# Two experts over all tokens: first layer in split float32r, sixteen parts over routing, lists and end, closing sum on VectorE

## The chip, the cores and the metric

The kernel runs on one core of one Trainium2 chip. Five engines work side by side, each through its own queue in order: TensorE (PE; its weight loads are shown as PEld), VectorE (DVE), ScalarE (ACT), GpSimd (POOL) and SyncE (SP), which issues most transfers. They wait for each other by semaphores only. The metric is the time on the device in microseconds, from the first to the last instruction; lower is better.

## The reference

One decoder layer on 32 sequences of 128 tokens with 128 channels (4096 tokens): self-attention, cross-attention with 16 heads over 77 keys, and a layer of experts, each followed by residual and layer normalization. The part that the change touches is the last, in which each of 8 experts takes its 1024 best tokens:

```python
scores = jax.nn.softmax(xt @ Wr, axis=-1)            # 4096 x 8
G, idx = jax.lax.top_k(scores.T, k)                  # k = 1024 tokens for each expert
X_in = xt[idx]
h = jax.nn.gelu(jnp.einsum('ekd,edh->ekh', X_in, W1) + b1[:, None, :], approximate=False)
X_e = jnp.einsum('ekh,ehd->ekd', h, W2) + b2[:, None, :]
contrib = (G[..., None] * X_e).reshape(E * k, D)
out = jnp.zeros((N, D), dtype=x.dtype).at[idx.reshape(-1)].add(contrib)
```

The result is the layer normalization of x + out.

## The kernel before

**Attention** goes over 16 pairs of sequences in software-pipelined steps (`first` = -2 to 16; steps 1 to 12 are a loop over four kinds of step, so all numbers of a kind repeat). In a step TensorE works for three pairs: self-attention of the next pair (prep), cross-attention of this one (cross), and the rest of the one before (post). Results go through a ring of four PSUM banks. A unit of work takes the next bank, and waits on `ring_free` of that bank until its last content has been copied out; whoever copies it adds one to `ring_free`. The post stage ends with x2 of the pair before, which TensorE transposes into ring bank 2 (unit "x2T"); ScalarE copies it to `xall`, where the transposed x2 of all tokens gathers. Three head products (308 columns) follow, and then `cross_out(0)`, whose unit takes the same bank 2. VectorE in the same step does, in this order: maximum and subtraction of the scores of the first sequence (`cross_max(0)`, `cross_sub(0)`), their sums, small work of self-attention, `cross_max(1)`, `cross_sub(1)`, `first_norm` (first layer normalization), `cross_sum(1)`. The exponentials between are ScalarE's.

**Routing.** Softmax gates from a router product (`router`, x2T times Wr). Then each expert's 1024th best gate is found in 15 rounds of a search: VectorE counts gates above three candidates, TensorE sums the counts with one small product, VectorE takes the next candidates. After the rounds VectorE makes one-hot matrices, from which TensorE makes the lists of tokens (`make_list`).

**Experts.** Seven experts are listed: POOL gathers their rows by indirect DMA (8 of 128 rows each), TensorE transposes them, takes the first layer (8 products of 512 columns, `hidden`), ScalarE the gelu, TensorE the second layer (`second_layer`), VectorE adds the bias and multiplies by the gate (`results`), POOL scatters the rows to DRAM, SP loads them back (`landed`), and VectorE adds them to `fin`, which holds x2 (`add_landed`). The eighth expert runs over all 4096 tokens instead, with a weight of 0 where it hadn't chosen a token. It is cut into 8 parts of 512 tokens: per part four chunks of the first layer (`dense_hidden`, one product of 512 columns each) and four result steps (`dense_result`, four products of 128 columns each). Six parts run in routing, two steps per round and the others around the lists, in an order counted by `dense(n)`; two run between listed experts. ScalarE copies a part's result from PSUM, and VectorE adds it to `fin` with its weight (`dense_add`: one addition of the bias on 512 columns and four weighted additions on 128).

**End.** TensorE adds `fin` and the last landed rows in PSUM by products with the identity; VectorE takes statistics per group of four sequences, POOL the power -1/2, ScalarE normalizes 28 sequences and VectorE the last four, and SP stores eight groups.

## Time and profile before

| | |
|---|---|
| time, median of 3 runs | 589.05 us (585.27 to 589.71) |
| profiled execution, span | 585.1 us |
| TensorE busy | 549.5 us (94%) |
| VectorE busy | 417.1 us (71%) |
| ScalarE busy | 327.3 us (56%) |
| POOL busy | 260.2 us (44%) |

A matmul of float32 shows as two instructions in the profile, so that x8 stands for four products. Durations of single instructions overlap; the start of one row to the start of the next is the better measure of what a product costs. Time in brackets at the end of a row is the engine's idle time before it, with what ended it.

### The profile page before, as it was taken

The page shows a single profiled execution, that of the slowest core. Times are in us where ns is not written, and L with a number is a line of the kernel's source. Part 1 is how long each engine was busy: PE and PEld are TensorE (multiplying, and loading weights), DVE is VectorE, ACT ScalarE, POOL GpSimd, SP SyncE. Part 2 cuts the span into 40 slices and gives each one's busy share as a digit, 9 for nine tenths or more (in the row PEclk, how much of TensorE's full clock was granted, in tenths as well). Part 3 has the DMA queues.
Part 4 walks back from the last instruction along what each step waited for, and adds up shares of the span by engine and source line. Part 5 has one row for each costly group of instructions (what it writes and reads, how often), then busy time and mean ns, then how long its engine had stood idle before and what let it go on. Part 6 is the DMA issues. An engine that isn't in the chain of part 4 may idle for free.

```text
span 585.1 us, 11240 instructions
## 1 busy us (share of the span) xinstructions
PE 549.5 (94%) x3477; PEld 427.6 (73%) x3477; DVE 417.1 (71%) x1051; ACT 327.3 (56%) x670; POOL 260.2 (44%) x368
## 2 busy tenths in 40 slices
PE   8999999999999999999999898998999999999880
PEld 7868787888888788788878676566676575668530
DVE  3686786787687688668877875788758845656753
ACT  3577776767777677776767543442333525443133
POOL 4123524434352443435243430002777777777732
PEclk9999999999999999999999998998999999999985
DMA  7033442232234023423312404900223443665652
GB/s 242 2 82 91 135 117 52 96 109 97 47 115 134 25 83 115 112 50 115 104 60 65 150 10 144 304 2 11 55 57 106 138 129 121 191 194 163 221 185 108
DMA packets 62151, 63.43 MB, mean 108 GB/s; under 512 B 11809, under 2 KB 48930, under 8 KB 61858
## 3 DMA queue, kind: packets, MB, share of 16 engines
q1 hardware_dynamic: 58096, 55.37, 30.8%
q0 software_dynamic: 3584, 7.58, 4.6%
q8 instruction: 20, 0.33, 0.2%
q14 instruction: 17, 0.14, 0.1%
q10 hardware_dynamic: 434, 0.02, 0.0%
HBM read 36.85 MB, written 26.08 MB: 108 GB/s over the span
## 4 chain that ended last, share of the span: by engine, by line
PE 77%; DVE 13%; ACT 4%; issue 2%; POOL 1%; DMA 1%; POOLq 0%; DVEq 0%; ACTq 0%
PE PS L1577 17%; PE PS L1635 10%; PE PS L1607 9%; PE PS L1908 8%; PE PS L1930 7%; PE PS L1623 5%; PE PS L1821 4%; PE PS L1831 4%; DVE pc L1395 2%; DVE csum L1158 1%; ACT shared L891 1%; DVE cmax L1147 1%; PE PS L1681 1%; PE PS L1675 1%; PE PS L1667 1%
## 5 line engine op out<-in xcount | busy, mean ns | idle before, releaser
L767 POOL TENSOR_TENSOR pn<-pc,crcp 128x512 f32<-128x512 f32 (+1 forms) x93 | 80.4, 891 | 69.3 <-DVE crcp L1161 69.3
L1035 ACT ACTIVATE shared<-PS,b1T 128x512 f32<-128x512 f32 x88 | 60.5, 687 | 85.7 <-PE PS L1821 49.5
L807 POOL DMA_INDIRECT shared<-table,idx x56 | 54.3, 970 | 64.5 <-DVE idx L1402 48.0
L1607 PE MATMUL PS<-shared,x1T 128*128 128x512 f32 (+1 forms) x192 | 72.4, 513 | 1.2 <-ACT x1T L906 1.0
L817 POOL DMA_INDIRECT spread<-pn,idx x56 | 62.0, 1107 | 17.6 <-issue 15.6
L1607 PEld LDWEIGHTS PS<-shared,x1T 128*128 128x128 f32 x192 | 35.0, 189 | 37.6 <-issue 35.2
L862 ACT ACTIVATE shared<-PS 128x308 f32<-128x308 f32 x120 | 47.5, 428 | 25.5 <-PE PS L1577 25.2
L1147 DVE TENSOR_REDUCE cmax<-PS 128x16 f32<-128x1232 f32 x31 | 44.7, 1441 | 20.8 <-PE PS L1607 20.4
L1158 DVE TENSOR_REDUCE csum<-pc 128x16 f32<-128x1232 f32 x31 | 44.4, 1431 | 19.4 <-ACT pc L874 19.4
L1908 PE MATMUL PS<-pT,w 128*128 128x512 f32 x112 | 53.6, 611 | 3.3 <-ACT pT L1030 3.3
L1930 PEld LDWEIGHTS PS<-w,shared 128*128 128x128 f32 x448 | 51.7, 192 | 3.6 <-issue 3.1
L1930 PE MATMUL PS<-w,shared 128*128 128x128 f32 x448 | 52.9, 276 | 0.1
L862 ACT ACTIVATE pT<-PS 128x512 f32<-128x512 f32 (+2 forms) x97 | 44.0, 526 | 14.2 <-PE PS L1623 14.1
L786 POOL TENSOR_TENSOR rs<-ve,mhalf 128x2 f32<-128x2 f32 x16 | 11.2, 702 | 79.9 <-DVE ve L1217 79.9
L1152 DVE TENSOR_TENSOR pc<-PS,cmax 128x1232 f32<-128x1232 f32 x31 | 44.6, 1437 | 0.6
L1577 PE MATMUL PS<-cT_hi,heads_hi 128*128 128x308 f32 x128 | 43.8, 342 | 1.0 <-DVE r L1186 0.7
L874 ACT ACTIVATE pc<-pc 128x1232 f32<-128x1232 f32 x31 | 38.2, 1231 | 10.0 <-DVE pc L1152 9.6
L1908 PEld LDWEIGHTS PS<-pT,w 128*128 128x128 f32 x112 | 17.8, 189 | 32.8 <-ACT shared L1035 19.8
L1623 PE MATMUL PS<-ident,pn 128*128 128x128 f32 (+1 forms) x320 | 40.7, 274 | 0.9 <-ACT shared L891 0.5
L1831 PEld LDWEIGHTS PS<-w2d,shared 128*128 128x128 f32 x256 | 32.8, 196 | 10.2 <-issue 9.6
L1635 PE MATMUL PS<-VOeven,pT 128*128 128x128 f32 (+1 forms) x320 | 38.5, 276 | 1.0 <-ACT pT L862 0.5
L1635 PE MATMUL PS<-shared,pT 128*128 128x128 f32 (+1 forms) x320 | 38.5, 275 | 0.5 <-ACT pT L862 0.5
(209 smaller groups left out, 1208.1 us busy)
## 6 DMA issues: line engine op xcount, KB each, us to landing
spread<-zeros SPq DMA_DIRECT2D x112, 128.0 KB, 2.0
shared<-spread SPq DMA_DIRECT2D x56, 256.0 KB, 4.3
xboth<-in_x SPq DMA_DIRECT2D x16, 256.0 KB, 2.7
w<-in_W SPq DMA_DIRECT2D x2, 1792.0 KB, 9.2
rest<-stage SPq DMA_DIRECT2D x56, 52.0 KB
table<-x SPq DMA_DIRECT2D x16, 128.0 KB, 1.9
fin<-table SPq DMA_DIRECT2D x1, 2048.0 KB, 18.2
out_x<-fin SPq DMA_DIRECT2D x8, 256.0 KB, 2.0
```

The costliest lines, as they stand in the source:

```text
L767: pool.tensor_tensor(pn[:, e, at_pn:at_pn + n * (b - a)].rearrange("p (h k) -> p h k", h=n), pc[:, e, :].rearrange("p (h k) -> p h k", h=H ...
L807: pool.indirect_dma_start(xg[:, e % 3, h, :], None, table, bass.IndirectOffsetOnAxis(ap=idx[:, e, h:h + 1], axis=0)).then_inc(gathered[e % ...
L817: pool.indirect_dma_start(spread[e], bass.IndirectOffsetOnAxis(ap=idx[:, e, h:h + 1], axis=0), ye[:, e % 2, h, :], None).then_inc(scattere ...
L862: act.activation(dst, src, ACT.Copy).then_inc(free[bank_of(at, name)], 1)
L1035: act.activation(hid[:, c, 512 * h:512 * h + 512], PS[:, HID_BANKS[k % len(HID_BANKS)], :], ACT.Gelu, bias=b1T[:, bias:bias + 1]).then_inc ...
L1577: i = pe.matmul(bank, a, b, start=(n == 0), stop=(n == len(pairs) - 1))
L1607: i = pe.matmul(PS[:, n, 0:b - a], x1T[:, e, :], A[:, 2 * A_SLOT[phase] + e, a:b], start=True, stop=True)
L1623: i = pe.transpose(bank[0:rows, (c - a) * P:(c - a + 1) * P], pn[:, e, n:n + rows], ident[:, :])
L1635: i = pe.matmul(bank[:, 0:P], pT[0:rows, e, c * P:(c + 1) * P], VO[par][0:rows, e, c, :], start=(c == 0), stop=(c == CH - 1))
L1831: i = pe.matmul(PS[:, 1 + h, s * P:(s + 1) * P], hid[:, c, 512 * h + s * P:512 * h + (s + 1) * P], w2d[:, c, :], start=(c == 0), stop=(c = ...
L1908: pe.matmul(PS[:, HID_BANKS[k % len(HID_BANKS)], :], w1[:, e, c * P:(c + 1) * P], xeT[:, 512 * h:512 * h + 512], start=True, stop=True).th ...
L1930: i = pe.matmul(y_bank(e, h, s), hid[:, c, (4 * h + s) * P:(4 * h + s + 1) * P], w2[:, e, c, :], start=(c == 0), stop=(c == FC - 1))
```

## The change

- Two experts (6 and 7) run over all tokens, six are listed. There are 16 parts: part u takes tokens of group u // 2 and expert 6 + u % 2. Eight run in routing, one each after listed experts 1 and 3, six at the end.
- The first layer of these parts is done in split float32r: `xall` is kept as a high and a low half (float32r each), as is w1d, and a chunk is three products, high x high, low weights x high, high weights x low. The router is done in the same way.
- So x2T is taken out of its ring bank in two steps: ScalarE writes the high half and no longer frees the bank; VectorE (`x2T_rest`) subtracts it from the bank, writes the low half, and frees the bank. It stands behind `first_norm`.
- POOL splits Wr at the start and w1d after attention.
- In routing, `dense(2 + r % 2)` follows each round's product: two steps in even rounds, three in odd ones.
- The results of parts go to a buffer `yd` of eight. At the end VectorE takes `dense_add` of parts 10 to 14, the landed rows of the last expert, statistics and normalization from `fin` in SBUF in an order written out; TensorE's closing sum is gone. The last part is added straight from PSUM.
- Buffers of attention now lie where later ones are, so that memory suffices.

```diff
-LISTED = E - 1
-DENSE = E - 1
-GROUPS_OF_FOUR = B // 4
-IN_ROUTING = 6
+LISTED = E - 2
+DENSES = E - LISTED
+PARTS = DENSES * B // 4
+IN_ROUTING = 8
+BETWEEN = {1: IN_ROUTING, 3: IN_ROUTING + 1}
+AT_END = IN_ROUTING + len(BETWEEN)
+KEPT = 8
...
+            pool.wait_ge(w1d_in, 16)
+            pool.tensor_copy(w1d[0][:, :, :], w1d_raw).then_inc(w1d_split, 1)
+            pool.wait_ge(w1d_split, 1)
+            pool.tensor_tensor(w1d[1][:, :, :], w1d_raw, w1d[0][:, :, :].bitcast(F32), ALU.subtract).then_inc(w1d_split, 1)
...
                 if post:
-                    copy(at, "x2T", xall[:, bass.ds(2 * (p - 1), 2), :].rearrange("p e t -> p (e t)"), bank("x2T")[:, 0:2 * P])
+                    ring_wait_full(act, at, "x2T")
+                    act.activation(xall[0][:, bass.ds(2 * (p - 1), 2), :].rearrange("p e t -> p (e t)"), bank("x2T")[:, 0:2 * P],
+                                   ACT.Copy).then_inc(x2T_hi, 1)
...
+                def x2T_rest():
+
+                    wait(dve, x2T_hi, p)
+                    ring_wait_full(dve, at, "x2T")
+                    two = bass.ds(2 * (p - 1), 2)
+                    dve.tensor_tensor(xall[1][:, two, :].rearrange("p e t -> p (e t)"), ring[bank_of(at, "x2T")][:, 0:2 * P],
+                                      xall[0][:, two, :].rearrange("p e t -> p (e t)").bitcast(F32),
+                                      ALU.subtract).then_inc(free[bank_of(at, "x2T")], 1)
...
                 if prep:
                     first_norm()
+                if post and cross:
+                    x2T_rest()
...
+            add_landed(LISTED - 2, 0, B // 4)
+            dense_add(10)
+            dense_add(11)
+            dense_add(12)
+            add_landed(LISTED - 1, 0, B // 4)
+            fin_stats(0)
+            fin_stats(1)
+            dense_add(13)
+            fin_stats(2)
+            fin_stats(3)
+            fin_stats(4)
+            fin_stats(5)
+            dense_add(14)
+            last_bias()
+            fin_stats(6)
+            last_add()
+            fin_stats(7)
...
-                        i = pe.matmul(small[:, b * E:(b + 1) * E], xall[:, b, :], wr[:, :], start=True, stop=True)
+                        i = products(small[:, b * E:(b + 1) * E], ((xall[0][:, b, :], wrs[0][:, :]), (xall[0][:, b, :], wrs[1][:, :]),
+                                                                   (xall[1][:, b, :], wrs[0][:, :])))
...
+                w_hi, w_lo = [t[:, d, c * P:(c + 1) * P] for t in w1d]
+                x_hi, x_lo = [t[:, 4 * g:4 * g + 4, :].rearrange("p b t -> p (b t)") for t in xall]
+                products(PS[:, HID_BANKS[k % len(HID_BANKS)], :],
+                         ((w_hi, x_hi), (w_lo, x_hi), (w_hi, x_lo))).then_inc(hid_full, 1)
...
-                    dense(2)
+                    dense(2 + r % 2)
...
+            for u in range(AT_END, PARTS):
+                if u < AT_END + 2:
+                    pe.wait_ge(ye_done, 2 * (LISTED - 1) + u % 2 + 1)
+                else:
+                    pe.wait_ge(dense_out, u - 1)
+                for n in range(FC):
+                    if u + 1 < PARTS:
+                        dense_hidden(end_hidden(u + 1) + n, u + 1, n)
+                    dense_result(end_hidden(u), u, u % 2, n)
```

VectorE in a looped attention step, before, from the statistics of `first_norm` (writing mv and ve) to the sum of the second sequence's exponentials (csum); pc holds the exponentials:

```order
L1210 BN_STATS st<-PS 128x6
L174 REGISTER_ALU
L1214 BN_AGGR mv<-st 128x2 [waits ln1_steps]
L1214 BN_AGGR mv<-st 128x2
L1217 TENSOR_SCALAR ve<-mv 128x2 [waits ln1_steps]
L1158 TENSOR_REDUCE csum<-pc 128x16 [waits cexp_done]
L1161 RECIPROCAL crcp<-csum 128x16 [waits csum_done]
```

The same place of the changed kernel:

```order
L1242 BN_STATS st<-PS 128x6
L177 REGISTER_ALU
L1246 BN_AGGR mv<-st 128x2 [waits ln1_steps]
L1246 BN_AGGR mv<-st 128x2
L1249 TENSOR_SCALAR ve<-mv 128x2 [waits ln1_steps]
L177 REGISTER_ALU [waits x2T_hi]
L1210 ISA [waits ring_full2]
L1210 TENSOR_TENSOR xall_lo<-PS,xall_hi 128x256
L1181 TENSOR_REDUCE csum<-pc 128x16 [waits cexp_done]
L1184 RECIPROCAL crcp<-csum 128x16 [waits csum_done]
```

Between the last operation of `first_norm` and the sum the subtraction has come in, with two register and wait instructions ahead of it.

TensorE in the changed kernel's looped step, the transposes of x2 (x_0); before, these rows and the next read the same but for their line numbers:

```order
L1834 MATMUL PS<-ident,x_0 128x128 [waits ring_free2,x2_done]
L1834 MATMUL PS<-ident,x_0 128x128
```

Behind them on TensorE, from the last of the head products (cT and heads) to the first products of `cross_out(0)` (out of pT):

```order
L177 REGISTER_ALU
L1597 MATMUL PS<-cT_hi,heads_hi 128x308 [waits ring_free1]
L1597 MATMUL PS<-cT_lo,heads_hi 128x308
L1597 MATMUL PS<-cT_hi,heads_lo 128x308
L1695 MATMUL PS<-shared,pT 128x128 [waits ring_free3,ring_free2]
L1695 MATMUL PS<-shared,pT 128x128 x3
L1695 MATMUL PS<-shared,pT 128x128 [waits ring_free0]
```

The first product of `cross_out(0)` waits on ring_free2, the bank that the x2T transposes filled; it was freed by ScalarE's copy and is now freed by VectorE's subtraction.

TensorE at the end of routing, before: from the last quarter of list 1 (out of pc and tokens) to the transposes of the first expert's gathered rows (in the tile named shared):

```order
L1889 MATMUL PS<-tokens,pc 128x16 [waits onehot_done]
L1889 MATMUL PS<-tokens,pc 128x16 x7
L1831 MATMUL PS<-w2d,shared 128x128 x12
L1900 MATMUL PS<-ident,shared 128x128 [waits gathered0_0,w2_in,w1_in]
```

And in the changed kernel a chunk and a result behind the list (four products of w2d are one result step):

```order
L1597 MATMUL PS<-xall_hi,w1d_hi 128x512 [waits hid_done]
L1597 MATMUL PS<-xall_hi,w1d_lo 128x512
L1597 MATMUL PS<-xall_lo,w1d_hi 128x512
L1898 MATMUL PS<-w2d,shared 128x128 [waits hid_done,dense_out]
L1898 MATMUL PS<-w2d,shared 128x128 x3
```

Its last chunk, the results behind it, and the first expert's transposes:

```order
L1597 MATMUL PS<-xall_hi,w1d_hi 128x512 [waits hid_done]
L1597 MATMUL PS<-xall_hi,w1d_lo 128x512
L1597 MATMUL PS<-xall_lo,w1d_hi 128x512
L1898 MATMUL PS<-w2d,shared 128x128 x4
L1898 MATMUL PS<-w2d,shared 128x128 [waits hid_done,dense_out]
L1898 MATMUL PS<-w2d,shared 128x128 x15
L1969 MATMUL PS<-ident,shared 128x128 [waits gathered0_0,w2_in,w1_in]
```

Three result steps (x12) have become four chunks and eight result steps; between the two pieces the pattern of a chunk and a result goes on.

VectorE at the end, before, from the last landed rows to the first statistics:

```order
L1460 TENSOR_TENSOR fin<-fin,shared 128x512 [waits landed_added,landed_in6]
L1460 TENSOR_TENSOR fin<-fin,shared 128x512 [waits landed_added,landed_in7]
L1506 BN_STATS stf<-PS 128x6 [waits fin_full,landed_added]
L1506 BN_STATS stf<-PS 128x6 x3
L1509 BN_AGGR mvf<-stf 128x2 [waits chain]
```

And in the changed kernel, from `dense_add(12)` into the landed rows of the last expert:

```order
L1469 TENSOR_TENSOR yd<-yd,b2b 128x512 [waits dense_added,landed_added,dense_out]
L1471 SCALAR_TENSOR_TENSOR fin<-yd,weight,fin 128x128 [waits chain]
L1471 SCALAR_TENSOR_TENSOR fin<-yd,weight,fin 128x128 x3
L1487 TENSOR_TENSOR fin<-fin,shared 128x512 [waits landed_added,landed_in0,dense_added]
L1487 TENSOR_TENSOR fin<-fin,shared 128x512 [waits landed_added,landed_in1]
```

The landed rows of the last expert now stand behind the addition of part 12, and the statistics read `fin` and wait for both.

## Rows read from the trace of the kernel before

**Rows 1.** Busy time by stage: window, then engines' busy us and count, PEclk, DMA, GB/s.

```profile
100.00:200.00 100.00, 99.70 (x639) 83.91 (x638) 76.36 (x173) 72.80 (x162) 41.44 (x70) 1.00 0.30 90
...
362.00:366.00 4.00, 3.45 (x6) 1.64 (x7) 2.35 (x11) 1.74 (x2) 0.00 (x0) 0.50 1.02 409
```

**Rows 2.** Timeline, TensorE: start us, us, line, tiles, count, idle before. Starts of experts.

```profile
419.82 3.89 PE L1908 MATMUL PS<-pT,w 128*128 128x512 f32 x8 [0.74 <-ACT pT L1030]
...
484.23 3.89 PE L1908 MATMUL PS<-pT,w 128*128 128x512 f32 x8 [1.26 <-ACT pT L1030]
...
504.05 7.66 PE L1908 MATMUL PS<-pT,w 128*128 128x512 f32 x16
...
519.56 7.66 PE L1908 MATMUL PS<-pT,w 128*128 128x512 f32 x16
...
545.89 4.11 PE L1930 MATMUL PS<-w,shared 128*128 128x128 f32 x32
```

**Rows 3.** Timeline, TensorE: cross_out(0) of two steps, and scores(0) of a next.

```profile
209.54 2.40 PE L1635 MATMUL PS<-VOeven,pT 128*128 128x128 f32 x20
...
214.46 2.33 PE L1607 MATMUL PS<-shared,x1T 128*128 128x512 f32 x6
...
271.86 2.40 PE L1635 MATMUL PS<-shared,pT 128*128 128x128 f32 x20
```

**Rows 4.** Timeline, VectorE: cmax(0), end of first_norm, csum(1), next cmax(0); another step's.

```profile
197.02 1.44 DVE L1147 TENSOR_REDUCE cmax<-PS 128x16 f32<-128x1232 f32 x1 [0.92 <-PE PS L1607]
...
211.06 0.17 DVE L1217 TENSOR_SCALAR ve<-mv 128x2 f32<-128x2 f32 x1
211.14 1.43 DVE L1158 TENSOR_REDUCE csum<-pc 128x16 f32<-128x1232 f32 x1
...
216.83 1.44 DVE L1147 TENSOR_REDUCE cmax<-PS 128x16 f32<-128x1232 f32 x1 [0.34 <-PE PS L1607]
...
272.80 0.17 DVE L1217 TENSOR_SCALAR ve<-mv 128x2 f32<-128x2 f32 x1
```

**Rows 5.** Timeline, VectorE, routing: a copy of 128x256 from PSUM.

```profile
363.25 0.42 DVE L1331 COPY gatesT<-PS 128x256 f32<-128x256 f32 x1 [0.84 <-PE PS L1855]
```

**Rows 6.** Chain that ended last, in order of time: start us, us, engine, line.

```profile
454.46 3.64 PE PS L1821 x8
...
459.35 3.89 PE PS L1908 x8
...
463.23 3.57 PE PS L1831 x32
```

**Rows 7.** Timeline, TensorE: float32r value products, single instructions.

```profile
201.39 0.48 PE L1577 MATMUL PS<-heads_hi,cmain_hi 128*128 128x512 f32 x1
201.71 0.40 PE L1577 MATMUL PS<-heads_hi,cmain_lo 128*128 128x512 f32 x1
201.95 0.39 PE L1577 MATMUL PS<-heads_lo,cmain_hi 128*128 128x512 f32 x1
```

**Rows 8.** Timeline, TensorE: the count product that closes two rounds.

```profile
391.20 0.18 PE L1864 MATMUL PS<-count,group 128*128 128x7 bf16 x1
...
393.23 0.18 PE L1864 MATMUL PS<-count,group 128*128 128x7 bf16 x1
```

**Rows 9.** Timeline, VectorE: dense add, landed add, statistics, last normalization.

```profile
439.14 0.68 DVE L1443 TENSOR_TENSOR xall<-xall,b2b 128x512 f32<-128x512 f32 x1
...
440.95 0.68 DVE L1443 TENSOR_TENSOR xall<-xall,b2b 128x512 f32<-128x512 f32 x1
...
536.25 4.89 DVE L1460 TENSOR_TENSOR fin<-fin,shared 128x512 f32<-128x512 f32 x8
...
571.62 0.88 DVE L1506 BATCH_NORM_STATS2 stf<-PS 128x6 f32<-128x128 f32 x4
...
573.10 0.88 DVE L1506 BATCH_NORM_STATS2 stf<-PS 128x6 f32<-128x128 f32 x4
...
575.71 1.36 DVE L1517 TENSOR_SCALAR fin<-PS,mvf,rsf 128x128 f32<-128x128 f32 x4 [1.06 <-POOL rsf L834]
```

More of the change, by code:

```diff
@@ L227, in decoder_layer @@
             wheadsT = set_up_only.enter_context(nc.sbuf_tensor("wheadsT", [P, 3, HEADS // 2, P], F32))
-        xall = sb("xall", [P, B, P])
+        xall_hi = sb("xall_hi", [P, B, P], F32R)
         wT = sb("wT", [P, 3, P])
         wvo = sb("wvo", [P, 2, P + 1])
+        xall_lo = sb("xall_lo", [P, B, P], F32R)
+        xall = [xall_hi, xall_lo]
+        wr = sb("wr", [P, E])
+        wrs = [sb(f"wr_{k}", [P, E], F32R) for k in ("hi", "lo")]
+        b1T = sb("b1T", [P, E * FC])
         with ExitStack() as attention:
@@ L243, in decoder_layer @@
             VOeven = part("VOeven", [P, 2 * HKP])
+            xboth = [part(f"xboth{k}", [P, 2, 2, P]) for k in range(2)]
+            xin = [t[:, 0, :, :] for t in xboth]
+            xT = [t[:, 1, :, :] for t in xboth]
+            cin = part("cin", [P, 4 * KEYS])
+            crin = part("crin", [P, REST])
+            crest = [part(f"crest_{k}", [P, REST], F32R) for k in ("hi", "lo")]
+            stage = part("stage", [REST, 2, 4 * P])
+            xbo = part("xbo", [P, 2, P])
+            qT = part("qT", [P, 2, P])
+            vs = part("vs", [P, 2, P + 1])
+            skey = part("skey", [P, 2])
+            smin = part("smin", [P, 2])
+            pself = part("pself", [P, 2, P])
+            ssum = part("ssum", [P, 2])
+            srcp = part("srcp", [P, 2])
+            pselfT = part("pselfT", [P, 2, P])
+            st1 = part("st1", [P, 2, 6])
+            mv1 = part("mv1", [P, 2, 2])
+            ve1 = part("ve1", [P, 2])
+            rs1 = part("rs1", [P, 2])
+            x1 = [part(f"x1_{k}", [P, 2, P]) for k in range(2)]
+            x1T = part("x1T", [P, 2, P])
         MT = [t[:, 0:HEADS, :] for t in halves]
@@ L348, in decoder_layer @@
         nmf = sb("nmf", [P, B])
-        w1d = sb("w1d", [P, F])
-        w2d = sb("w2d", [P, FC, P])
-        weight = sb("weight", [P, B])
+        w1d = [sb(f"w1d_{k}", [P, DENSES, F], F32R) for k in ("hi", "lo")]
+        w2d = sb("w2d", [P, DENSES, FC, P])
+        weight = sb("weight", [P, DENSES, B])
         self_in = sem("self_in")
@@ L483, in hidden_before, with end_hidden @@
         def hidden_before(e):
-            return FC * IN_ROUTING + 2 * FC * e + FC * sum(e > k for k in TAIL)
-        TAIL = {1: IN_ROUTING, 2: IN_ROUTING + 1}
+            return FC * IN_ROUTING + 2 * FC * e + FC * sum(e > k for k in BETWEEN)
+        def end_hidden(u):
+            return hidden_before(LISTED) + FC * (u - AT_END)
         CONSTS = 21
@@ L805, in gather @@
                     pool.wait_ge(ye_done, 2 * (e - 2))
-                for h in range(first, end):
+                for h in range(SB):
                     pool.indirect_dma_start(xg[:, e % 3, h, :], None, table,
@@ L1473, in _ @@
                 make_idx(e)
-            for e in range(LISTED - 1):
+            for e in range(LISTED):
                 if e + 3 < LISTED:
@@ L1484, in _ @@
                     add_landed(e - 2, B // 8, B // 4)
-                if e < 2:
-                    for k in range(IN_ROUTING // 2 * e, IN_ROUTING // 2 * (e + 1)):
-                        dense_add(k, 0)
-                if e - 1 in TAIL:
-                    dense_add(TAIL[e - 1], B // 4 * (e - 1))
-            add_landed(LISTED - 3, 0, B // 4)
-            last_results()
-            add_landed(LISTED - 2, 0, B // 4)
+                for u in ((0, 1, 2), (3, 4, 5), (6, 7), (8,), (), (9,))[e]:
+                    dense_add(u)
             def fin_shift(c):
@@ L1533, in _, with products @@
             pe.wait_ge(consts, 4)
+            def products(bank, pairs):
+                for n, (a, b) in enumerate(pairs):
+                    i = pe.matmul(bank, a, b, start=(n == 0), stop=(n == len(pairs) - 1))
+                return i
             def set_up_unit(k):
@@ L1573, in done @@
                     i.then_inc(full[bank_of(at, name)], 1)
-                def products(bank, pairs):
-                    for n, (a, b) in enumerate(pairs):
-                        i = pe.matmul(bank, a, b, start=(n == 0), stop=(n == len(pairs) - 1))
-                    return i
                 def heads(which):
```

300 lines of the change are left out of this document (139 added, 161 removed).

## The prediction

> **What bounds the kernel now.** I read the busy time by stage first: between 100 and 200 us TensorE works 99.70 of 100 us at a granted clock of 1.00 [rows 1]. So whatever TensorE gets to do or to wait for during attention is paid in full. Then the timelines, engine by engine, and the chain of waits for prices. Up to 362 us there is attention (16 steps, one per pair of sequences), up to 419.82 routing [rows 2], then seven listed experts, whose last second layer starts at 545.89 and takes about 4.1 us [rows 2], so TensorE's own work on experts is over at 550.0. The last 35.1 of the 585.1 us are scatter, landing, closing sum and normalization. This tail is what the six closing parts are laid over.
>
> The profiled execution takes 585.1 us, which is the fastest of the three times; their median is 589.05. I make the sum against 585.1 and carry the difference over at the end.
>
> **A. The new x2T handover, 12 looped steps.** Before, ScalarE copied the transposed x2 out of its ring bank right after TensorE had written it, and cross_out(0) started at 209.54 without idle time ahead of it [rows 3]. Now ScalarE writes only the high half, and the bank is given back by VectorE's subtraction, which stands behind first_norm. The order excerpt of TensorE's looped step shows who waits: the first matmul of cross_out(0) asks for ring_free2, the bank of x2T, and only three head products lie between. In the step shown VectorE's last operation of first_norm starts at 211.06 and the next one at 211.14 [rows 4]. The subtraction is 128x256 with one operand in PSUM; its nearest row is a 128x256 copy from PSUM at 0.42 us [rows 5]. In the loop two register and wait instructions stand in front of it, which I put at 0.1. So the bank is free at 211.14 + 0.1 + 0.42 + 0.05 for the semaphore = 211.7, against 209.54: a wait of 2.2 us.
>
> Is the wait made good later? VectorE's work from cmax(0) at 197.02 to 211.14 is one chain: cmax, subtraction, ScalarE's exp, sum, and then back to back without a gap. It starts when TensorE's scores(0) end. From cross_out(0) to the scores of the next step TensorE needs 214.46 - 209.54 = 4.9 us and the scores another 2.3 [rows 3]; nothing of it can move ahead. So the loop of one step becomes 197.02 to 211.7 on VectorE, then 7.3 us on TensorE to the next cmax(0) (216.83 before, [rows 4]): 22.0 us where there were 19.8. The wait comes back in every step. The other looped steps repeat four kinds; one kind has an earlier first_norm, 272.80 against a cross_out(0) at 271.86 [rows 3, 4], which gives 0.94 + 0.08 + 0.57 = 1.6. So 9 x 2.1 + 3 x 1.6 = 23.7, less 0.5 for small waits for x1 that vanish behind it: **+23.2** (bounds 20 and 26).
>
> **B. The last four steps and the gates.** Here heads and prep run out, TensorE waits for VectorE anyhow, and the new wait replaces part of another. Nothing: 0; all of it: 4 x 2.1 = 8.4. I take half, **+4**. The 32 router products become three of 8 columns each; the trace has no such product, and I leave them at nothing, with 1.4 us to either side. POOL's split of w1d (two operations on 1024 columns) is wanted when TensorE begins its dense chunks; POOL stands idle there (0.00 of 4 us, [rows 1]) and has its last attention work behind it before the gates are made. Nothing, at most 1.
>
> **C. Price of a part.** A float32 chunk of the first layer takes 3.64 / 4 = 0.91 us, a result step (four 128x128 products) 3.57 / 4 = 0.89 [rows 6]. A split chunk is three float32r products of 512 columns. The same shape stands in the value products, at 201.39, 201.71 and 201.95 [rows 7], so 0.32 for the first one after float32 work, then 0.23 each: 0.78 after float32, 0.69 otherwise. One chunk and one result: 0.78 + 0.89 = 1.67 us, against 1.80 before. A whole part is 6.7 us.
>
> The Trainium skill (TensorE: Matmul & The Clock Gate, Back-to-back issue gap) gives N / 2.4 + 2.5 ns for a warm matmul, 216 ns for 512 columns, and knows no extra after a float32 product. By it a chunk would be 0.65 us, and about 30 chunks on the path some 4 us cheaper in all, an estimate. The rows here show 0.23 and 0.32.
>
> **D. Rounds.** A round runs 391.20 to 393.23 = 2.03 us [rows 8] and VectorE sets it; TensorE has one chunk and one result, 1.83. With 1.67 the even rounds stay at 2.03. Odd rounds have three steps: chunk, result, chunk 2.45 + 0.04 (four rounds, +0.46) or result, chunk, result 2.56 + 0.04 (three rounds, +0.57): +3.55. In the first two rounds TensorE's products ran at half clock (0.50 between 362 and 366, [rows 1]) and held VectorE up; cheaper chunks give back 0.9. **+2.65** (0 to 3.6).
>
> **E. End of routing.** While lists are made VectorE's one-hots set the pace, so cheaper chunks bring nothing. Behind list 1 there were 3 result steps, 2.67 us; now 4 chunks and 8 results: 4 x 0.78 + 8 x 0.89 = 10.24. **+7.6**. Hidden(0,0) starts at 427.4 instead of 419.82 (the other shifts apart).
>
> **F. Listed stretch.** It was 550.0 - 419.82 = 130.2. Experts 0 and 1 took 459.35 - 419.82 = 39.5 [rows 2, 6], and in them are four dense chunks from 454.46 and a 1.25 us wait for ScalarE behind them, 4.9 in all; with cheaper chunks ScalarE's gelus end 0.6 earlier: 38.9. e2 loses its own chunks, so it is like e3 before, 504.05 - 484.23 = 19.8. e3 is e4 before (519.56 - 504.05 = 15.5) plus chunks and wait (4.45): 20.0. e4 is 15.5 + 3.57 = 19.1. e5: 7.5 + 3.57 + four chunks 3.05 + 3.57 = 17.7. Sum 115.4, end at 542.8. So one expert less saves **-14.8**.
>
> **G. The end.** Parts 10 to 15 follow. TensorE needs 5 x 6.7 + 3.57 = 37.1, end 579.9. But VectorE's order decides: dense_add(12) stands ahead of add_landed(5), and needs part 12: 542.8 + 3 x 6.7 + 0.85 (ScalarE's copy) = 563.75. Earlier work of VectorE (add_landed(4), parts 10, 11) is 4.9 + 2 x 1.81 = 8.5 us and fits in front. The last expert's landed rows were ready, at latest, 571.62 - 550.0 = 21.6 us behind its second layer [rows 2, 9]; now that is 564.4, and they are asked for at 565.6. So part 12 is what is waited for. From there VectorE has, by [rows 9]: dense_add 1.81 three times (12, 13, 14); eight landed adds 4.9; stats of groups 0 to 6 at 1.48, 10.4 in all; last_bias and last_add 2.3; then from stats(7) to the end of the last normalization 577.07 - 573.10 = 3.97. Sum 27.0, so 590.8. From the last normalization to the end of the span it was 585.1 - 577.07 = 8.0, and stays. End 598.8, which is **+13.7** against 585.1. ScalarE's 28 normalizations start near 577 and end before VectorE.
>
> **Sum.** 585.1 + 23.2 + 4 + 2.65 + 13.7 = 628.7. (E and F are inside G.) Without the x2T handover the same change would be 602: eight more parts cost more than one listed expert and the covered tail give back.
>
> **Rivals.**
> - *The bank is free in time* (10%): VectorE's place behind first_norm isn't reached late after TensorE's new rhythm, or the delay is absorbed before the next scores. For it: VectorE idles 0.34 to 0.92 us ahead of cmax(0) [rows 4]. Against: that idle is behind the wait, not before it. Then 585.1 + 2.65 + 13.7 = 601.5, up to 606.
> - *More than the plain wait* (7%): a late cross_out(0) makes the second normalization late, which goes over POOL and VectorE to the x2 that the next transposes need. If it falls behind by 1 us more in each of 13 steps: 642 and more.
> - *Not slower* (3%): TensorE takes up the handover and the extra steps in idle time, so that only the covered tail counts. The tail after the last expert was 35.1; all of B, D, E would have to vanish: 419.8 + 115.4 + 37.1 + about 13 for a tail bound by TensorE = 585. It decides once TensorE has 40 us of idle before 550; but it is idle 585.1 - 549.5 = 35.6 us in the whole span, most of it in the tail. Against it speaks the 99.70 of 100 too.
>
> **Numbers.** Forecast 80%: 628.7 on the profiled execution; the median of before lies 4 us over its profile, so I name 631. The range holds the bounds of A to G (20 to 26, 0 to 8.4, 0 to 3.6, some 3 us for G and 1.4 for the router) and a little of the second rival: 616 to 643. About 1% is what a measurement of this kernel tells from no change. Faster 0.01, same 0.03, slower 0.96.
>
> **What would show it.** Right: in the looped steps a wait of cross_out(0) of about 2 us released by VectorE's subtraction, cmax(0) to cmax(0) near 22 us where it was 19.8; attention some 25 us longer; TensorE idle in steady steps for the first time. Rounds alternating 2.03 and 2.5. Twelve steps of 10.2 us ahead of the first transposes. At the end VectorE without a gap from dense_add(12) on, TensorE done some 11 us before the last normalization. Wrong: if attention keeps its length, A falls and the time is about 602. If VectorE has gaps at the end, a landing or ScalarE sets it. If a chunk comes to 0.65 us, C is off by 3 to 4 us.

## The result, and the profile after

| | before | changed |
|---|---|---|
| median, us | 587.16 (4 runs) | 644.25 (4 runs, 642.9 to 645.85) |
| profiled execution, span | 585.1 | 642.1 |
| TensorE busy | 549.5 (94%) | 579.9 (90%) |
| VectorE busy | 417.1 (71%) | 429.1 (67%) |

The changed kernel takes 1.095 of the time before (95% interval 1.088 to 1.101), 57 us more. I had forecast 631 (616 to 643): the direction was right, the size 13 us short. By stages of the two profiled executions, where the boundaries are the first maximum of a step on VectorE, the first and the last count product of the search, hidden(0,0), and the end of the last listed second layer:

| stage | before | changed | difference | forecast |
|---|---|---|---|---|
| to the last maximum of attention | 346.5 | 377.9 | +31.3 | +27.2, with the next row |
| last maximum to first count product | 19.9 | 29.9 | +10.0 | |
| 14 rounds of the search | 28.8 | 32.7 | +3.8 | +2.65 |
| last count product to hidden(0,0) | 24.6 | 32.3 | +7.7 | +7.6 |
| hidden(0,0) to the last listed second layer | 130.2 | 116.2 | -13.9 | -14.8 |
| from there to the end | 35.1 | 53.2 | +18.1 | +20.9 |

First the waits of TensorE over the whole execution (line waited for: us in all, times, the longest), the changed kernel:

```profile
PE PS L1695 <- DVE xall_lo L1210: 27.5, 14, 3.0
PE PS L1977 <- ACT pT L1047: 3.3, 3, 1.3
```

L1695 is cross_out, L1210 the new subtraction. Before, the same product started without idle time ahead of it [rows 3]. Its place in one step on TensorE (start us, us, line, tiles, count, idle before), changed kernel:

```profile
225.13 0.30 PE L1597 MATMUL PS<-cT_hi,heads_lo 128*128 128x308 f32 x1
227.50 2.50 PE L1695 MATMUL PS<-VOeven,pT 128*128 128x128 f32 x20 [2.07 <-DVE xall_lo L1210]
```

and on VectorE, the end of first_norm, the subtraction, the sum; before, the second row was not there [rows 4]:

```profile
226.79 0.17 DVE L1249 TENSOR_SCALAR ve<-mv 128x2 f32<-128x2 f32 x1
227.02 0.42 DVE L1210 TENSOR_TENSOR xall_lo<-PS,xall_hi 128x256 f32 x1
227.36 1.42 DVE L1181 TENSOR_REDUCE csum<-pc 128x16 f32<-128x1232 f32 x1
```

The head product's last piece starts at 225.13, the subtraction ends at 227.44, and cross_out(0) starts at 227.50. The next step's first maximum shows the period: 212.75 to 234.68 us, 21.9 where it was 19.8.

In two of the twelve looped steps the period went to 24.9 us, where the forecast's terms give 21.1 + 2.1 = 23.2. There the same products run slower behind the wait. TensorE in one of them, and then the windows around it (window, busy us of PE, PEld, DVE, ACT, POOL with counts, granted clock, DMA share, GB/s):

```profile
249.30 4.12 PE L1695 MATMUL PS<-shared,pT 128*128 128x128 f32 x20 [2.04 <-DVE xall_lo L1210]
```

```profile
248.00:250.00 2.00, 0.70 (x5) 0.70 (x6) 1.76 (x6) 1.04 (x4) 0.70 (x1) 0.93 0.00 0
250.00:252.00 2.00, 2.00 (x11) 2.00 (x11) 1.40 (x4) 0.00 (x0) 1.04 (x2) 0.50 0.00 0
252.00:254.00 2.00, 2.00 (x12) 1.81 (x12) 0.50 (x2) 0.00 (x0) 1.52 (x3) 0.72 0.00 0
```

Twenty instructions take 4.12 us that took 2.40 before [rows 3], at a granted clock of 0.50, the lower of the two levels (1.2 and 2.4 GHz), after 2 us in which TensorE stood idle.

### The profile page after: what moved, and what is told of

Its sections match the earlier page's. It is cut to its first block, busy times and chain, and to the rows that moved or that the text cites. A ratio compares the mean times of both kernels' runs of the same rounds, so it can differ in the third digit from the quotient of the medians.

```text
span 642.1 us, 11830 instructions
## 1 busy us (share of the span) xinstructions
PE 579.9 (90%) x3741; PEld 477.1 (74%) x3741; DVE 429.1 (67%) x1086; ACT 347.7 (54%) x699; POOL 247.2 (38%) x356
## 3 DMA queue, kind: packets, MB, share of 16 engines
q1 hardware_dynamic: 54640, 51.17, 26.4%
## 4 chain that ended last, share of the span: by engine, by line
PE 51%; DVE 32%; issue 8%; ACT 6%; DMA 1%; DVEq 1%; SPq 0%; POOLq 0%; POOL 0%
PE PS L1597 15%; PE PS L1695 8%; PE PS L1990 6%; PE PS L1977 6%; DVE cmax L1170 6%; PE PS L1898 6%; PE PS L1667 6%; DVE csum L1181 3%; DVE pc L1175 3%; ACT pc L889 3%; DVE pc L1430 2%; DVE PS L1272 1%; DVE shared L1264 1%; DVE above L1375 1%; DVE PS L1236 1%
## 5 line engine op out<-in xcount | busy, mean ns | idle before, releaser
L1052 ACT ACTIVATE shared<-PS,b1T 128x512 f32<-128x512 f32 x112 | 77.0, 688 | 99.2 <-PE PS L1597 71.0
L827 POOL DMA_INDIRECT shared<-table,idx x48 | 46.3, 965 | 73.1 <-DVE idx L1437 59.4
L1898 PEld LDWEIGHTS PS<-w2d,shared 128*128 128x128 f32 x512 | 65.4, 194 | 5.2 <-issue 1.0
L1898 PE MATMUL PS<-w2d,shared 128*128 128x128 f32 x512 | 67.4, 279 | 0.0
L837 POOL DMA_INDIRECT spread<-pn,idx x48 | 51.7, 1078 | 26.2 <-DVE pn L1450 13.1
L1695 PE MATMUL PS<-shared,pT 128*128 128x128 f32 (+1 forms) x320 | 44.6, 302 | 12.4 <-DVE xall_lo L1210 11.9
L1695 PE MATMUL PS<-VOeven,pT 128*128 128x128 f32 (+1 forms) x320 | 40.7, 284 | 16.1 <-DVE xall_lo L1210 15.6
L1695 PEld LDWEIGHTS PS<-shared,pT 128*128 128x128 f32 (+1 forms) x320 | 42.3, 215 | 14.4 <-DVE xall_lo L1210 13.6
L1695 PEld LDWEIGHTS PS<-VOeven,pT 128*128 128x128 f32 (+1 forms) x320 | 38.5, 198 | 18.1 <-DVE xall_lo L1210 17.3
L1977 PE MATMUL PS<-pT,w 128*128 128x512 f32 x96 | 46.1, 612 | 3.3 <-ACT pT L1047 3.3
L1990 PEld LDWEIGHTS PS<-w,shared 128*128 128x128 f32 x384 | 44.4, 192 | 3.0 <-issue 2.9
L1990 PE MATMUL PS<-w,shared 128*128 128x128 f32 x384 | 45.1, 276 | 0.0
```

The costliest lines, as they stand in the source:

```text
L1052: act.activation(hid[:, c, 512 * h:512 * h + 512], PS[:, HID_BANKS[k % len(HID_BANKS)], :], ACT.Gelu, bias=b1T[:, bias:bias + 1]).then_inc ...
L1695: i = pe.matmul(bank[:, 0:P], pT[0:rows, e, c * P:(c + 1) * P], VO[par][0:rows, e, c, :], start=(c == 0), stop=(c == CH - 1))
L1898: i = pe.matmul(y, hid[:, c, 512 * h + s * P:512 * h + (s + 1) * P], w2d[:, u % DENSES, c, :], start=(c == 0), stop=(c == FC - 1))
L1977: pe.matmul(PS[:, HID_BANKS[k % len(HID_BANKS)], :], w1[:, e, c * P:(c + 1) * P], xeT[:, 512 * h:512 * h + 512], start=True, stop=True).th ...
L1990: i = pe.matmul(PS[:, 1 + h, s * P:(s + 1) * P], hid[:, c, (4 * h + s) * P:(4 * h + s + 1) * P], w2[:, e, c, :], start=(c == 0), stop=(c = ...
```

## The experiments

Ratios are against the kernel before on the same chip, with 95% intervals. The first four runs below were made on a chip on which the kernel before took 623.1 us; there TensorE waited in short pieces with no releaser (issue) in the stretch of the experts, so these runs are read by their stages in attention and gates, which show no such pieces. Of the kernel before there is no profile on that chip, but the run with one expert has its attention and gates unchanged: they took 293.8 and 19.8 us there. "Attention" below is from step 1's first maximum to the last maximum: 293.9 us before (52.60 to 346.51), 325.9 in the changed kernel (51.96 to 377.85).

### The subtraction earlier in VectorE's queue

```diff
                 if cross and first < PAIRS - 1:
                     cross_sub(1)
+                    if post:
+                        x2T_rest()
...
-                if post and cross:
+                if first == PAIRS - 1:
                     x2T_rest()
```

> The changed kernel, with VectorE's subtraction of x2T moved from behind first_norm to right behind cross_sub(1), 2.9 us earlier in its queue; nothing else. Theory A (the late return of ring bank 2 is what makes attention longer: 31 us by the time of cmax in the last step, 585.1 against 642.1 in span): the bank is free within 0.2 us of when cross_out(0) wants it, the 2 us waits in front of cross_out(0) go, first_norm comes 0.35 us later in a step; cmax(0) to cmax(0) about 20 and 21.3 us, attention 26 to 31 us shorter, span 613 to 616. With the waits the stretches at half clock in two of the looped steps (about 1.7 us each) should go too. Rival (the added subtraction and ScalarE's writing of the high half make the steps longer by themselves): less than 10 us comes back, over 630.

Measured: 1.041 (1.036 to 1.046) of the kernel before on its chip. Attention took 299.9 us: 26 of the 32 us are back. The two steps at half clock are gone as well (periods 21.5 us). In the list of TensorE's waits the line of cross_out no longer stands among the largest; of its 14 waits for the subtraction one is left:

```profile
PE PS L1960 <- issue: 9.8, 13, 1.9
PE PS L1979 <- ACT pT L1047: 4.9, 3, 2.4
PE PS L1992 <- issue: 4.6, 5, 1.2
PE PS L1979 <- ACT shared L1052: 2.2, 1, 2.2
...
PE PS L1697 <- DVE xall_lo L1210: 1.2, 1, 1.2
```

So theory A holds; the rival does not. The span of 647.7 us is no test of the 613 to 616, because of the chip; the run with both fixes below is. The gates stretch was not mended: 30.7 us.

### The late return alone, on the kernel before

```diff
-                    copy(at, "x2T", xall[:, bass.ds(2 * (p - 1), 2), :].rearrange("p e t -> p (e t)"), bank("x2T")[:, 0:2 * P])
...
                 if prep:
                     first_norm()
+                if post and cross:
+                    x2T_copy()
```

> The kernel before, in float32 and with one expert over all tokens as it was; only the copy of x2T out of ring bank 2 is taken from ScalarE and given to VectorE behind first_norm, where the changed kernel has its subtraction. Theory A: that alone brings the wait of about 2.1 us ahead of cross_out(0) into each looped step, cmax(0) to cmax(0) near 21.9 and 23.3 us, one step in four up to 24.9 where the clock falls; time 610 to 617. Rival (the wait is harmless without the other parts of the change): under 595.

Measured: 1.062 (1.058 to 1.066), 40 us more on that chip. Attention 327.2 us, 33.2 more than before, with no high and low half, one expert over all tokens, and nothing else changed but that the copy is VectorE's work and no longer ScalarE's. TensorE's waits:

```profile
PE PS L1640 <- DVE xall L1220: 27.1, 14, 3.0
```

This is nearly the same sum, over the same 14 steps, as in the changed kernel. Who frees the bank, and when, makes the attention part of the loss. (Of the 40 us, 33 are attention; I did not settle what the other 7 are on that chip.)

### The router with one product per block

```diff
-                        i = products(small[:, b * E:(b + 1) * E], ((xall[0][:, b, :], wrs[0][:, :]), (xall[0][:, b, :], wrs[1][:, :]),
-                                                                   (xall[1][:, b, :], wrs[0][:, :])))
+                        i = products(small[:, b * E:(b + 1) * E], ((xall[0][:, b, :], wrs[0][:, :]),))
```

> The changed kernel with one product per block of the router (high x high) in place of three: the two with a low half are left out, so gates are less exact. From the last cmax of attention to the first count product it took 29.9 us in the changed kernel and 19.9 before. Theory R (64 more router products of 0.11 us at full and 0.21 us at half clock, and a granted clock of 0.50 over some 23 us around them): 32 products take some 4 us where 96 took about 17; 7 to 10 us come back, 632 to 635. Rival R2 (the 10 us come from VectorE's x2T_rest standing ahead of the last sums, a wait of 2.98 us, and from waits for bank 2): 3 us or less come back, over 639.

Measured: 1.072 (1.069 to 1.075) on that chip. From the last maximum to the first count product 21.4 us, where it was 29.9 and, before, 19.9: 8.5 of the 10 us are back, as theory R said. (Other executions with all 96 products took 27.1 and 30.7 us there, so the gain is 5.7 to 9.3 us.) R2 falls by this and again below. What a product costs is in two rows of the changed kernel's TensorE, first at full, then at half clock:

```profile
376.81 0.25 PE L1597 MATMUL PS<-wr_hi,xall_hi 128*128 128x8 f32 x1
376.92 0.25 PE L1597 MATMUL PS<-wr_lo,xall_hi 128*128 128x8 f32 x1
...
381.40 0.35 PE L1597 MATMUL PS<-wr_hi,xall_hi 128*128 128x8 f32 x1
381.61 0.35 PE L1597 MATMUL PS<-wr_lo,xall_hi 128*128 128x8 f32 x1
```

Start to start 0.11 and 0.21 us. The kernel before had the router in float32; these rows of its TensorE were there to be read:

```profile
356.41 2.74 PE L1645 MATMUL PS<-wr,xall 128*128 128x8 f32 x24
359.00 0.42 PE L1772 MATMUL PS<-ident,x 128*128 128x128 f32 x2
```

24 instructions in 2.59 us from the start of one row to the start of the next: 0.108 each, two for a block, 0.22. Three products of 0.111 are 0.33. So 32 blocks cost 32 x 0.12 = 3.8 us more at full clock. That is not the whole: this run has half the router instructions of the kernel before and still takes 1.5 us longer. The rest goes with the clock. Over this stretch the mean granted clock was 0.86 before, 0.64 in the changed kernel and 0.77 here, and the executions with three products follow it: 25.1 us at 0.80 (with the wide weights below), 27.1 at 0.71, 29.9 at 0.64, 30.7 at 0.62. What takes the clock down there stays open.

### One expert, its last two parts at the end

```diff
-        TAIL = {1: IN_ROUTING, 2: IN_ROUTING + 1}
+        TAIL = {}
...
+            for c in range(FC):
+                dense_hidden(last + c, IN_ROUTING, 0, c)
+            pe.wait_ge(ye_done, blocks_through(LISTED - 1, SB - 1))
+            for g in range(IN_ROUTING, B // 4):
+                for n in range(FC):
+                    if g + 1 < B // 4:
+                        dense_hidden(last + FC * (g + 1 - IN_ROUTING) + n, g + 1, (g + 1) % 2, n)
+                    dense_result(last + FC * (g + 1 - IN_ROUTING), g, g % 2, n)
```

(with statistics and normalization from fin, as in the changed kernel)

> The kernel before, with seven listed experts and one over all tokens in float32 as it was, but the last two of its 8 parts are moved from between listed experts to the end, and the closing sum goes to VectorE (landed rows and statistics group by group from fin, additions of parts 6 and 7 ahead of group 6). It takes from the change only its use of the tail. Each part between experts cost TensorE 3.64 + 1.26 + 3.57 = 8.5 us, so the last listed second layer ends 17 us earlier, near 533; rows land 17 us earlier, at 544 to 553; parts 6 and 7 take TensorE until about 549. VectorE then has 8 x 2.1 + 2 x 1.8 = 20.4 us from 544, the last normalization is at 567, end at 575 (572 to 580). Rival (landing or VectorE's chain gives it all back): 583 or more. If one expert over all tokens laid into the tail is faster and two are slower, the tail holds two or three parts of 6.4 to 7.2 us, not six.

Measured: 1.022 (1.018 to 1.027). TensorE's waits there had 29 us put down to issue, in the stretch of the listed experts:

```profile
PE PS L1939 <- issue: 14.1, 27, 1.2
PE PS L1898 <- issue: 12.7, 14, 1.9
```

So it was run again, on a chip on which the kernel before took 585.9 us.

> The kernel before with its last two parts in the tail, as in the run before. There it was 1.022 of the kernel before where the sum said 0.983, with 29 us of idle time of TensorE put down to issue between 440 and 580 us. Theory I (that idle time, which this chip or its instruction supply brings into straight code, hit it harder): where the kernel before takes 587 us, TensorE has none of it and the kernel takes 574 to 580. Theory V (the tail has no room: landing or VectorE's chain binds): it is at 587 or over there too.

Measured: 593.5 us, 1.012 (1.008 to 1.016). Theory I falls: without the issue waits it is slower too. V is right about what bounds the tail: VectorE waits for the first landed rows until 559.32 and then runs without a gap up to the usual 1.06 us ahead of the last normalization, while TensorE is done at 563.9. But the sum had counted that chain, and the tail took 41.8 us where the sum had 42 (533 to 575). What the sum had wrong is the listed stretch: it did not get shorter at all. Windows over it, before and then this kernel (columns as above):

```profile
419.82:550.00 130.18, 127.34 (x852) 88.65 (x852) 84.87 (x153) 51.94 (x79) 100.14 (x97) 1.00 0.45 137
```

```profile
419.17:549.31 130.14, 118.81 (x773) 82.88 (x774) 81.17 (x143) 45.74 (x69) 100.33 (x97) 0.96 0.44 138
```

TensorE has 8.5 us less busy time (and slower products, at a mean clock of 0.96), and the stretch still takes 130.1 us. The waits of TensorE name what took the place of its work, the gathered rows:

```profile
PE PS L1909 <- DMA shared<-table,idx: 10.7, 6, 4.2
```

and POOL has the two groups that make them, in this kernel (line, form, count, busy us, mean ns, idle before):

```profile
L817 POOL DMA_INDIRECT spread<-pn,idx x56 | 60.6, 1082 | 17.1 <-issue 15.8 <-DVE pn L1434 0.6 <-DVE pn L1421 0.6
L807 POOL DMA_INDIRECT shared<-table,idx x56 | 55.2, 985 | 64.7 <-DVE idx L1408 48.2 <-issue 16.2 <-DVE pn L1434 0.3
```

Each is followed by 0.30 us of issue, so a listed expert costs POOL 8 x (1.08 + 0.98 + 0.6) = 21.3 us (the first gathers lie ahead of the stretch), more than the 15.5 us that TensorE needs for an expert without a dense part [rows 2]. In the stretch of the kernel before, POOL's idle time ahead of these two groups is 27.7 us of issue and 2.3 us of waits for VectorE. With seven listed experts POOL is a second bound at 130 us, and the two dense parts between them were free work in its shadow. The tail then held them at a price, 41.8 us where there were 35.1: the end moved from 585.1 to 591.1.

### Once more the changed kernel, on that chip

> The changed kernel once more, unchanged, so that the others of this call have it on their own chip: in the call before, the kernel before took 623 us where it took 587 in the first comparison, with TensorE idle in short pieces that nothing released (put down to issue) in the stretch of the listed experts alone. Attention and routing have no such pieces. Expected: a ratio near 1.095 where the kernel before takes 587; cmax(0) to cmax(0) 21.9, 24.9, 23.4, 21.9 as before.

Measured: 646.2 us, 1.102 (1.098 to 1.107). The waits for the bank are again 27.5 us in 14 steps, but the periods differ from run to run: six of the looped steps had stretches at half clock here, two in the first profile, and attention took 330.6 us, not 325.9. The wait is fixed; what the clock adds to it is not.

### The router's products widened

```diff
-                        i = products(small[:, b * E:(b + 1) * E], ((xall[0][:, b, :], wrs[0][:, :]), (xall[0][:, b, :], wrs[1][:, :]),
+                        i = products(small[:, b * E:b * E + WIDE], ((xall[0][:, b, :], wrs[0][:, :]), (xall[0][:, b, :], wrs[1][:, :]),
```

> The changed kernel, with the router's weights padded by zeros from 8 to 64 columns: the same 96 products, each with 8 times the columns, written over each other in rising order so that each block keeps its 8. Theory K (the granted clock falls to half around the narrow products, and that is most of the 10 us that the last attention step and the gates take longer): it stays at 1.00 for most of that stretch, and 4 to 7 us come back although no product is saved, 637 to 640 where the changed kernel takes 644. Theory N (it is the number of products alone, 0.11 us each): no gain, and wider products can only be slower, 644 to 647.

Measured: 645.6 us, 1.100 (1.095 to 1.105), against 646.2: no difference that can be measured. Its gates stretch took 25.1 us at a mean clock of 0.80, the unchanged kernel's on the same chip 27.1 at 0.71. That leans the way of theory K, with 2 us and not 4 to 7; since unchanged code gave 27.1, 29.9 and (with the early subtraction) 30.7 us there, it is not shown. What the run does show is that eight times the columns cost nothing.

### Both fixes together

The subtraction behind cross_sub(1), as in the first diff, and the wide router; and in the last step that has them, the last sums go ahead:

```diff
                 if first == PAIRS - 1:
                     last_sums(0)
                     last_sums(1)
+                    x2T_rest()
```

> The changed kernel with x2T's subtraction right behind cross_sub(1) in the steps, behind the last sums in the last step that has them, and with the router's weights 64 columns wide. Expected from the two effects: 26 to 28 us from attention and 5 to 8 from the gates, 609 to 613 where the changed kernel takes 644; what then remains over the kernel before, 20 to 26 us, is rounds (3.8), the end of routing (7.7) and the listed stretch with the end (9.5), and attention about 2. Under 600 would mean that those weren't priced right.

Measured: 613.9 us, 1.047 (1.042 to 1.052), where the changed kernel took 646.2: 32 us back. Attention 300.0 us, gates 25.1 us. Putting the last sums in front brought nothing to the gates stretch (25.1 in both this and the wide router alone), which speaks against R2 once more. What remains over the kernel before, 27.5 us by the spans (612.6 and 585.1): attention 6.1, gates 5.2, rounds 3.0, end of routing 9.2, listed stretch and end 4.1.

### Who frees the bank

```diff
+                    wait(act, x2T_lo, p)
+                    act.activation(x2c[:, :], bank("x2T")[:, 0:2 * P], ACT.Copy).then_inc(free[bank_of(at, "x2T")], 1)
```

> On top of the run with both fixes (613.9 us, steps of 20.6, 20.1, 21.5, 21.6 us): ScalarE copies the transposed x2 a second time, as float32 into SBUF, and that frees ring bank 2; VectorE's subtraction reads the copy and stands where the changed kernel has it, behind first_norm. Theory A' (only the time at which the bank comes back matters, not where the subtraction stands): no wait of 2 us ahead of cross_out(0), steps as with both fixes or 0.3 us shorter, since first_norm no longer has the subtraction in front of it: 609 to 614. Rival (a subtraction behind first_norm delays the sum and the second normalization as much): steps over 21.5 us throughout, over 625.

Measured: 613.9 us, 1.044 (1.037 to 1.052). Attention 300.0 us, the same as with the early subtraction, although the subtraction is again behind first_norm. So its place costs nothing once the bank no longer hangs on it; theory A' holds. The 6 us that attention still takes over the kernel before stay too, in both variants, so the order does not make them. The 0.42 us that each of 15 steps has more on VectorE come to 6.3 us; that these are the cause fits in size but was not tested.

### Two steps a round

```diff
-                    dense(2 + r % 2)
+                    dense(2)
```

> On top of both fixes: two dense steps in each round of the search, where odd rounds had three. The seven steps move behind list 1. From the rows: rounds get 7 x 0.55 = 3.8 us shorter, the end of routing 4 x 0.78 + 3 x 0.81 = 5.5 us longer, so 1 to 2 us slower, 615 to 616; a gain would mean that steps behind list 1 are hidden.

Measured: 616.5 us, 1.047 (1.039 to 1.055), not to be told from 613.9 by that interval. By stages: rounds 29.2 us where both fixes had 31.8, end of routing 37.9 where it had 33.8. The trade is 2.6 against 4.2 where 3.8 against 5.5 had been worked out. In the rounds the first one took 0.7 us more here (2.79 and 2.09); the end of routing took 32.3 to 33.8 us in other runs with the same code there, the chip of the first four left out.

### The router in two products

```diff
+                        pe.matmul(small[:, 2 * E * b:2 * E * (b + 1)], xall[0][:, b, :], wrs[:, 0:2 * E], start=True, stop=False)
+                        i = pe.matmul(small[:, 2 * E * b:2 * E * b + E], xall[1][:, b, :], wrs[:, 0:E], start=False, stop=True)
```

> On top of both fixes, but with the router in two products in place of three (high x with high and low weights side by side in 16 columns, low x with the high weights) and a copy and an addition on VectorE per batch of gates. Theory N (number of products, 0.11 us each at full and 0.21 at half clock): 32 products less, of which some 24 lie on the path, 2.6 to 5 us, less 2 x 0.6 us of VectorE: 1.5 to 4 us faster, 610 to 612. If narrow products pull the clock down, part of it goes back: no change.

Measured: 614.2 us, 1.043 (1.037 to 1.049): no gain. TensorE was busy for 3.0 us less in the gates stretch (19.1 against 22.1), but that took 25.1 us as before, at a clock of 0.73 in place of 0.80, and VectorE had 2.7 us more. The run also gives up the wide weights, so it does not tell the count of products from their columns.

### All of it

The last diff and the one on who frees the bank, together.

> bank_by_act and router_two together, the best that I know to make of two experts over all tokens: 606 to 611, still some 20 us over the kernel before, which is what one more expert over all tokens costs (51 us of TensorE for 8 parts, against one listed expert and about 17 us of a tail better filled).

Measured: 613.5 us, 1.040 (1.033 to 1.047), 2.5 us over the range that I expected. Its gates stretch was the shortest of the versions with the full router, 22.8 us at a clock of 0.82. No version with two experts over all tokens comes within 20 us of the kernel before, and the kernel before stays the fastest of all that ran.

## Why the prediction was right, and where it was short

**What bounds the kernel** was right for attention, and for the listed stretch only half of it: TensorE and POOL both fill its 130 us. I read the busy share of POOL (44% of the whole) and never added up its queue between 420 and 550 us, where it is busy for 100 us and issuing for most of the rest. The forecast got away with it: with six listed experts POOL waited 19 us for VectorE in that stretch, so TensorE alone set its length.

**A, the handover.** The mechanism is shown from both sides: moved earlier or freed by ScalarE it goes, put alone into the kernel before it comes. The wait was 2.07 us in the step of which I said 2.2. For the 12 looped steps I had +23.2; they took 28.4 us more (246.3 and 274.7). The four kinds took 2.2, 2.5, 1.7 and 2.1 us more in the first turn of the loop, 25.5 for three turns, and two steps had 1.6 more by the clock. The twelve waits themselves add up to 23.2 us, the number of the forecast, but the steps grew by more. 2 us are missing by rule: with both fixes, and no such wait left in them, the same 12 steps still took 251.6 us, so the term had work in it that I priced at nothing. The other 3 us are the clock: a wait costs more than its length where the clock falls behind it.

**B, the last steps and the gates**, is the step that failed. The steps 13 to 15 took 3.6 us more (2.0 in the second execution), which is near the 4 of the text. But I had left the router at nothing, with 1.4 us to either side, and said that the trace has no such product. It had one that was near enough, 0.108 us for an instruction of 8 columns, and three for two of these is 3.8 us at full clock; with the clock at half for much of the stretch it took 10.0 us more. This is 10 of the 13 us that I was short. The count of products is shown as a cause by the run with one product; how the 6 us beyond the 3.8 divide between products at half clock and other work at half clock was not taken apart. The Trainium skill (TensorE: Matmul & The Clock Gate, Back-to-back issue gap) gives about 81 ns for a weight load with a product of 128 columns in a sustained stream; the 8 columns here took 110 ns. By that figure, 32 blocks would be 7.8 us for three products, an estimate; the rows give 10.6.

**C, the price of a part.** A chunk and a result take 1.59 us, not 1.67. TensorE at the end, changed kernel:

```profile
609.39 0.48 PE L1597 MATMUL PS<-xall_hi,w1d_hi 128*128 128x512 f32 x1
609.70 0.40 PE L1597 MATMUL PS<-xall_hi,w1d_lo 128*128 128x512 f32 x1
609.94 0.39 PE L1597 MATMUL PS<-xall_lo,w1d_hi 128*128 128x512 f32 x1
610.17 1.05 PE L1898 MATMUL PS<-w2d,shared 128*128 128x128 f32 x8
610.98 0.48 PE L1597 MATMUL PS<-xall_hi,w1d_hi 128*128 128x512 f32 x1
```

The chunk has its 0.78 from start to start, the result only 0.81: I read the extra that the first float32r product has behind float32 work as the end of that work, which I had counted in both. Without it a chunk is 0.70, 0.23 for each product as the rows of before had it [rows 7], so the 216 ns of the Trainium skill (TensorE: Matmul & The Clock Gate, Back-to-back issue gap) was also a little low here. A part is 6.4 us.

**D, rounds.** Even rounds 2.04, odd rounds 2.4 and 2.6 us, as said; the seven odd ones come to 3.55 us over 2.03 each, the sum's number. The 0.9 us that the first rounds should give back did not come: from count product to count product before had only 0.4 us to give (2.40 and 2.05), and the first round ran at half clock here too and took 2.64 us.

**E, F.** +7.7 where I had +7.6, with 10.23 us for the last four chunks and eight results (461.10 to 471.33) where I had 10.24, and 116.2 us where I had 115.4.

**G, the end.** The order was read rightly. dense_add(12) waits for its part on ScalarE's copy, behind an idle time of VectorE, and from there VectorE runs without a gap up to the 1.06 us ahead of the last normalization, which stood there before too [rows 9]. VectorE, changed kernel:

```profile
608.70 0.69 DVE L1469 TENSOR_TENSOR yd<-yd,b2b 128x512 f32<-128x512 f32 x1 [4.51 <-ACT yd L1060]
609.43 1.14 DVE L1471 SCALAR_TENSOR_TENSOR fin<-yd,weight,fin 128x128 f32<-128x128 f32 x4
610.61 4.91 DVE L1487 TENSOR_TENSOR fin<-fin,shared 128x512 f32<-128x512 f32 x8
...
633.98 1.11 DVE L1577 TENSOR_SCALAR fin<-fin,mvf,rsf 128x128 f32<-128x128 f32 x4 [1.06 <-POOL rsf L849]
```

19.8 us from the last listed second layer to dense_add(12) (21.0 in the text, by C), 26.4 from there to the last normalization's end (27.0), 7.0 to the end of the span (8.0). TensorE's last product ends at 624.5, 10.6 us ahead of that end (about 11). The term was 2.8 us too high.

The sum: 14.1 short in attention and gates, 2.1 in D, E and F, 2.8 over in G; 628.7 became 642.1. (To 628.7 I added 2.3 us, not the 4 by which the text has the median above its profile; measured, the medians lie 2.1 above both profiles.) The number came out where I had put the rival *more than the plain wait*, but not by its mechanism, a late second normalization: a wait for x2 is not among the seven longest of TensorE, and the 12 periods without the clock's part grew by 25.5 us, of which 23.2 are the plain waits. The range ended 1 us below the measured median since the gates had a bound of 1.4 us where the rows allowed 3.8 at full clock and twice that at half clock.

## What to carry to other kernels

A buffer that several engines pass on in a tight loop is held until the last reader in the slowest queue has come to it: when a copy gets a second reader, put that reader where its engine stands at that time, or let the first one copy the data out and free the buffer. Price small products by the instruction, not by their columns, and count them. Work moved from between transfers only brings what the engine that issues the transfers leaves: add up that engine's queue over the stretch before you take work off another.

## What the runs showed of the hardware

- Waits of 2 us on TensorE in otherwise full steps were followed in some steps, not in all and not in the same ones from run to run, by 3 to 4 us at a granted clock of 0.50; 20 instructions took 4.12 us in place of 2.40. Six of 12 looped steps had it in one execution of the changed kernel, two in another.
- Products of 8 and of 64 columns with a new 128x128 weight each followed each other alike, 0.11 us from start to start at a granted clock of 1.00; the wide ones made no measurable difference to the whole.
- One chip ran attention in the same time as the others and the stretch of listed experts more slowly: the kernel before took 623.1 us there, 585.9 to 589.6 elsewhere. TensorE idled in pieces of 0.2 to 1.9 us that nothing released. Where that comes from stays open.
- An indirect transfer of 128 rows keeps POOL for 0.98 us (gather) or 1.08 us (scatter), and 0.30 us more pass before the next.
